# Channel mix's key and value weights split earlier, beside the first cross attention batch, with the receptance product put first

## The reference, cut to what matters

```python
# cross attention (layer 4), each of the 8 batches by itself
q = query @ Wq + bq; k = key @ Wk + bk; v = value @ Wv + bv
attn = softmax((q k^T + q rel_k^T) / sqrt(32))
x = (attn v + attn rel_v) @ Wo + bo
# channel mix (second half of layer 5), H = 4 * 512
xc = _ln(x, ln2_g, ln2_b)
xx2 = _shift(xc)
xk2 = xc * cm_k + xx2 * (1 - cm_k)
xr2 = xc * cm_r + xx2 * (1 - cm_r)
kk = square(relu(xk2 @ ffn_Wk.T))      # (tokens, 2048)
kv = kk @ ffn_Wv.T
x = x + sigmoid(xr2 @ ffn_Wr.T) * kv
```

## Time and profile before

| | us |
|---|---|
| median of 3 runs | 1688.79 (1688.48 to 1689.01) |
| the profiled execution | 1689.68 |
| its span, first to last instruction | 1687.9 |
| cross attention, period 0 (units of the first batch) | 541.9 to 633.7 |
| channel mix, from its first product to its last block | 1523.7 to about 1655 |

### The profile page before, as it was taken

How to read it: one execution, slowest core, us unless ns; L and a number is a source line. 1 busy time by engine, 2 the same in 40 slices (tenths; PEclk the granted TensorE clock), 3 DMA queues, 4 the chain that set the end, 5 groups by cost and what they waited for, 6 DMA issues and landing times. The chain is left out here.

```text
span 1687.9 us, 26535 instructions
## 1 busy us (share of the span) xinstructions
PE 1471.6 (87%) x11120; PEld 1060.0 (63%) x11120; DVE 773.1 (46%) x1333; ACT 466.4 (28%) x772; POOL 557.9 (33%) x315
## 2 busy tenths in 40 slices
PE   8788977477988999999999999999998896936796
PEld 3556755243444778778787787788776673415573
DVE  2455279989435341332322323222232315978913
ACT  0323301031111115243242433324243431303302
POOL 6102057656323032122122122231232324617701
PEclk9779975788998999999999999999999998967997
DMA  5300030010101411111111111111012016003000
GB/s 233 149 1 1 0 137 1 0 69 0 75 0 64 147 51 57 52 34 53 39 42 51 39 48 42 38 52 57 30 42 78 22 57 256 0 0 119 1 0 25
DMA packets 50101, 91.29 MB, mean 54 GB/s; under 512 B 28600, under 2 KB 41664, under 8 KB 46912
## 3 DMA queue, kind: packets, MB, share of 16 engines
q1 hardware_dynamic: 49984, 89.60, 15.1%
HBM read 79.89 MB, written 9.70 MB: 53 GB/s over the span
## 5 line engine op out<-in xcount | busy, mean ns | idle before, releaser
L1074 POOL TENSOR_TENSOR ctx_hi<-ctx_raw,one 128x1536 fp32r<-128x1536 f32 (+1 forms) x36 | 102.9, 2858 | 617.5 <-DMA ctx_raw<-in_ctx 426.0
L1328 DVE TENSOR_TENSOR V<-PS,vbias 128x512 f32<-128x512 f32 (+1 forms) x104 | 71.9, 691 | 338.0 <-PE PS L1114 337.8
L1256 ACT COPY ET<-PS 128x512 f32<-128x512 f32 (+1 forms) x224 | 129.6, 585 | 299.1 <-PE PS L1170 295.4
L1359 DVE TENSOR_SCALAR_CACHE_REDUCE E<-PS 128x384 f32<-128x384 f32 (+1 forms) x256 | 131.8, 571 | 159.6 <-PE PS L1147 159.0
L1170 PE MATMUL PS<-ident,E 128*128 128x128 f32 (+1 forms) x832 | 127.3, 278 | 8.8 <-ACT ET L1256 8.8
L1077 POOL TENSOR_TENSOR ctx_raw_r<-ctx_raw,ctx_hi 128x1536 fp32r<-128x1536 f32 (+1 forms) x36 | 131.2, 3644 | 2.8
L1114 PE MATMUL PS<-ctx_raw_r,wk_hi 128*128 128x384 f32 (+1 forms) x512 | 128.6, 355 | 0.0
L1114 PE MATMUL PS<-wv_lo,ctx_hi 128*128 128x512 f32 (+1 forms) x416 | 125.9, 405 | 0.0
L1114 PE MATMUL PS<-ctx_hi,wk_hi 128*128 128x384 f32 (+1 forms) x512 | 122.9, 361 | 2.5 <-POOL ctx_raw_r L1077 2.5
L1263 ACT ACTIVATE E<-E,peak 128x1601 f32<-128x1601 f32 x64 | 103.5, 1623 | 64.8 <-DVE peak L1364 64.8
L1114 PE MATMUL PS<-wv_hi,ctx_hi 128*128 128x512 f32 (+1 forms) x416 | 120.5, 411 | 0.8 <-issue 0.8
(11 more groups left out here) (283 smaller groups left out, 2383.3 us busy)
## 6 DMA issues: line engine op xcount, KB each, us to landing
ctx_raw<-in_ctx SPq DMA_DIRECT2D x27, 768.0 KB, 4.4
ctx_raw<-in_ctx_first SPq DMA_DIRECT2D x9, 900.0 KB, 4.6
rel_scr<-rel_out SPq DMA_DIRECT2D x8, 640.0 KB, 3.8
fwk<-in_fwk SPq DMA_DIRECT2D x1, 4096.0 KB, 25.4
fwv<-in_fwv SPq DMA_DIRECT2D x1, 4096.0 KB, 12.7
corr<-rel_scr SPq DMA_DIRECT2D x64, 48.0 KB
p_scr<-E SPq DMA_DIRECT2D x16, 192.0 KB, 2.3
near<-p_scr SPq DMA_DIRECT2D x64, 48.0 KB
```

The lines of the kernel that those rows point to most:

```text
L1074: nc.gpsimd.tensor_tensor(ctx_hi[r][:, :, 0:n], ctx_raw[r][:, :, 0:n], one[:].unsqueeze(1).broadcast_to([P, KC, n]), ALU.mult).then_inc(S[ ...
L1256: nc.scalar.copy(ET[0:n, j % ET_RING, :], src[0:n, :]).then_inc(S["et_out"], 1)
L1328: v.tensor_tensor(V[0:rows, at % V_RING, :], bank(4 + NUMBER[unit] % 2)[0:rows, :], vbias[0:rows, :], ALU.add).then_inc(S["v_out"], 1)
L1359: v.tensor_scalar(E[:, p, k0:k0 + n], bank(r)[:, 0:n], 1.0, None, ALU.mult, ALU.max, accum_out=tops[:, p, c:c + 1]).then_inc(S["s_out"], 1)
```

## The change

The key and value weights of channel mix are no longer split there. They are cut into 32 pieces of 128 x 512 (256 KB each; 16 of keys, 16 of values), and each goes through the first batch's period of cross attention: SP loads it into a ring of four buffers (laid over ET, which is unused until period 1), ACT rounds it, DVE takes its rest, and SP stores both parts to a DRAM tensor, `split_scr`. The load of piece i + 4 waits for both stores of piece i. On ACT and DVE a piece stands in the list ahead of the copies of "its" unit; 26 units have one piece; units 9, 19 and 28 have two, unit 28 the pieces 30 and 31 (`PIECES_AFTER`). On SP pieces 0 to 7 are stored one behind each relative store, 8 to 14 behind `load_ctx(2)`, 15 to 21 behind `load_ctx(3)` and ahead of `load_corr(1)`, 22 to 26 behind `load_ctx(4)` and 27 to 31 behind `load_ctx(5)`. The first use of ET and of YT in period 1 waits for all stores.

In channel mix the parts are loaded: the keys' lo part in `cross_output`, the keys' hi part in four DMAs, and both value parts at the start of the block (12 MB there, in place of 4 MB). ACT, DVE and POOL lose their splits, the mix for receptance is made first, and PE makes the receptance product ahead of the 16 groups.

```diff
@@ -901,6 +901,8 @@
 
 
 PERIODS = [(p, p - 1, period(p)) for p in range(B + 1)]
+PIECES, PIECE_RING = 2 * HC, 4
+PIECES_AFTER = [range(i * PIECES // len(UNITS[0]), (i + 1) * PIECES // len(UNITS[0])) for i in range(len(UNITS[0]))]
...
@@ -912,6 +914,7 @@
 
 
 
+    s.split_scr = nc.dram_tensor("split_scr", [2, PIECES, P, D], F32, kind="Internal").ap()
...
+    et_at = m.at
...
+    yt_at = m.at
     s.YT = m.tensor("YT", [P, KC, TOK])
+    over_et, over_yt = Region(nc, et_at), Region(nc, yt_at)
+    piece_raw = over_et.tensor("piece_raw", [P, PIECE_RING, D])
+    piece_lo, piece_hi = over_et.rounded("piece_raw"), over_yt.tensor("piece_hi", [P, PIECE_RING, D], F32R)
...
+
+    def load_piece(sp, i):
+
+        r = i % PIECE_RING
+        if i >= PIECE_RING:
+            sp.wait_ge(piece_stored[r], 32 * (i // PIECE_RING))
+        src = s.dram["fwk"][:, i].rearrange("p c n -> p (c n)") if i < HC else s.dram["fwv"][:, i - HC]
+        sp.dma_start(piece_raw[:, r, :], src).then_inc(piece_loaded[r], 16)
+
+    def store_piece(sp, i):
+
+        r = i % PIECE_RING
+        sp.wait_ge(S["piece_hi"], i + 1)
+        sp.dma_start(s.split_scr[0, i], piece_hi[:, r, :].bitcast(F32)).then_inc(piece_stored[r], 16)
+        sp.wait_ge(S["piece_lo"], i + 1)
+        sp.dma_start(s.split_scr[1, i], piece_lo[:, r, :].bitcast(F32)).then_inc(piece_stored[r], 16)
+        if i + PIECE_RING < PIECES:
+            load_piece(sp, i + PIECE_RING)
...
+            for i in range(PIECE_RING):
+                load_piece(sp, i)
             for b in range(B):
                 sp.wait_ge(S["rel_out_act"], 2 * (b + 1))
                 sp.wait_ge(S["rel_out_dve"], 2 * (b + 1))
                 sp.dma_start(rel_scr[b].rearrange("a p k -> p a k"),
                              rel_out[b % 2][:].rearrange("p o r k -> p (o r) k")).then_inc(rel_stored[b % 2], 16)
+                for i in PIECES_AFTER[b]:
+                    store_piece(sp, i)
             load_corr(sp, 0)
             sp.wait_ge(S["p_zeroed"], 16)
+            stored = PIECES_AFTER[B - 1][-1] + 1
             for p, ba, items in PERIODS:
                 for c in range(NCH):
                     q = p * NCH + c
                     if 2 <= q:
                         load_ctx(sp, q)
+                    if p == 0 and c >= 2:
+                        for i in range(stored, stored + 7):
+                            store_piece(sp, i)
+                        stored += 7
+                    if p == 1 and c < 2:
+                        for i in range(stored, (stored + PIECES) // 2 if c == 0 else PIECES):
+                            store_piece(sp, i)
+                        stored = (stored + PIECES) // 2
                     if ba >= 0 and c == {B - 1: 3, B: 2}.get(p, 1):
                         exchange_near(sp, ba)
                     if c == 3 and p + 1 < B:
@@ -1253,6 +1294,9 @@
                 act.wait_ge(S["t_ps"], T_GROUPS * b + j + 1)
                 if b * P_GROUPS + kt >= 2:
                     act.wait_ge(S["pv_done"], b * P_GROUPS + kt - 1)
+                elif j == 0:
+                    for r in range(PIECE_RING):
+                        act.wait_ge(piece_stored[r], 32 * (PIECES // PIECE_RING))
                 nc.scalar.copy(ET[0:n, j % ET_RING, :], src[0:n, :]).then_inc(S["et_out"], 1)
 
...
+            def piece_round(i):
+                r = i % PIECE_RING
+                act.wait_ge(piece_loaded[r], 16 * (i // PIECE_RING + 1))
+                nc.scalar.copy(piece_hi[:, r, :], piece_raw[:, r, :]).then_inc(S["piece_hi"], 1)
+
             for p, ba, items in PERIODS:
                 for kind, k in items:
+                    if p == 0 and kind == "u" and k % 2:
+                        for i in PIECES_AFTER[k // 2]:
+                            piece_round(i)
...
+                if b == 0:
+                    for r in range(PIECE_RING):
+                        dve.wait_ge(piece_stored[r], 32 * (PIECES // PIECE_RING))
...
+            def piece_rest(i):
+                r = i % PIECE_RING
+                dve.wait_ge(S["piece_hi"], i + 1)
+                v.tensor_tensor(piece_lo[:, r, :], piece_raw[:, r, :], piece_hi[:, r, :].bitcast(F32),
+                                ALU.subtract).then_inc(S["piece_lo"], 1)
+
             for p, ba, items in PERIODS:
                 for kind, k in items:
+                    if p == 0 and kind == "u" and k % 2:
+                        for i in PIECES_AFTER[k // 2]:
+                            piece_rest(i)
                     if kind == "u" and k % 2:
                         unit = UNITS[p][k // 2]
                         if unit[0] == "v":
@@ -1407,6 +1471,7 @@
     s.b8 = Region(nc, nc.sbuf_usable_end // 32 * 32 - 4 * HC * KC * P)
...
 def cross_output(nc, sem, s, nm, nm2):
...
-            sp.dma_start(s.fwk[:], s.dram["fwk"]).then_inc(s.loaded["fwk"], 16)
+            sp.dma_start(s.fwk_lo[:].bitcast(F32).rearrange("p g c n -> p g (c n)"),
+                         s.split_scr[1, 0:HC].rearrange("g p n -> p g n")).then_inc(s.loaded["fwk"], 16)
...
+    fwk_lo, fwk_hi = s.fwk_lo, m.tensor("fwk_hi", [P, HC, KC, P], F32R)
...
-            sp.dma_start(fwv[:], s.dram["fwv"]).then_inc(S["l_v"], 16)
+            for j in range(4):
+                gs = slice(j * GROUP, (j + 1) * GROUP)
+                sp.dma_start(hidden_hi[:, gs].bitcast(F32), s.split_scr[0, gs].rearrange("g p n -> p g n")).then_inc(l_k[j], 16)
+            sp.dma_start(fwv_hi[:].bitcast(F32), s.split_scr[0, HC:PIECES].rearrange("g p n -> p g n")).then_inc(l_v_hi, 16)
+            sp.dma_start(fwv_lo[:].bitcast(F32), s.split_scr[1, HC:PIECES].rearrange("g p n -> p g n")).then_inc(l_v_lo, 16)
...
-            nc.gpsimd.memset(one[:], 1.0).then_inc(S["one"], 1)
             tr.pool(pool, xa, diff)
-            pool.wait_ge(S["one"], 1)
-            pool.wait_ge(S["l_v"], 16)
-            for g in range(HC):
-
-                nc.gpsimd.tensor_tensor(fwv_hi[:, g], fwv[:, g], one[:].broadcast_to([P, D]), ALU.mult).then_inc(S["v_split"], 1)
-                pool.wait_ge(S["v_split"], 2 * g + 1)
-                nc.gpsimd.tensor_tensor(fwv_lo[:, g], fwv[:, g], fwv_hi[:, g].bitcast(F32), ALU.subtract).then_inc(S["v_split"], 1)
...
         @block.tensor
         def _(pe):
             tr.tensor(pe, nm)
+            pe.wait_ge(s.loaded["fwr"], 16)
+            pe.wait_ge(S["mixed_r"], KC)
+            pe.wait_ge(tr.ready, KC)
+            for t in range(NT):
+                linear_to_tokens(nc, bank(t), flat(xr[:]), t, s.fwr, 0, D).then_inc(S["r_ps"], 1)
+            pe.wait_ge(s.loaded["fwk"], 16)
             pe.wait_ge(S["x_lo"], KC)
             for g in range(HC):
-                pe.wait_ge(S["k_lo"], g + 1)
+                pe.wait_ge(l_k[g // GROUP], 16)
...
-            pe.wait_ge(s.loaded["fwr"], 16)
-            pe.wait_ge(S["mixed"], 2 * KC)
-            pe.wait_ge(tr.ready, KC)
-            for t in range(NT):
-                linear_to_tokens(nc, bank(t), flat(xr[:]), t, s.fwr, 0, D).then_inc(S["r_ps"], 1)
-            pe.wait_ge(S["v_split"], 2 * HC)
+            pe.wait_ge(l_v_hi, 16)
+            pe.wait_ge(l_v_lo, 16)
             pe.wait_ge(S["h_lo"], HC)
...
         @block.scalar
         def _(act):
             tr.scalar(act, xa)
-            act.wait_ge(s.loaded["fwk"], 16)
-
-            def key_weights(g):
-                nc.scalar.copy(fwk_hi[:, g], fwk[:, g]).then_inc(S["k_hi"], 1)
...
-            for g in range(AHEAD):
-                key_weights(g)
             for c in range(KC):
                 act.wait_ge(S["mixed"], c + 1)
                 nc.scalar.copy(xk_hi[:, c], xk[:, c]).then_inc(S["x_hi"], 1)
+            for t in range(NT):
+                act.wait_ge(S["r_ps"], t + 1)
+                nc.scalar.activation(gate[:, t, :], bank(t), ACT.Sigmoid).then_inc(S["gate_in"], 1)
...
-                if g + AHEAD < HC:
-                    key_weights(g + AHEAD)
...
                     round_hidden(g - 1)
             round_hidden(HC - 1)
-            for t in range(NT):
-                act.wait_ge(S["r_ps"], t + 1)
-                nc.scalar.activation(gate[:, t, :], bank(t), ACT.Sigmoid).then_inc(S["gate_in"], 1)
...
-            def key_weights(g):
-                dve.wait_ge(S["k_hi"], g + 1)
-                v.tensor_tensor(fwk_lo[:, g], fwk[:, g], fwk_hi[:, g].bitcast(F32), ALU.subtract).then_inc(S["k_lo"], 1)
-
...
+            tr.vector(dve, xa, diff, ((vec("cm_r"), xr),), S["mixed_r"])
             tr.vector(dve, xa, diff, ((vec("cm_k"), xk),), S["mixed"])
-            for g in range(AHEAD):
-                key_weights(g)
             for c in range(KC):
...
-            tr.vector(dve, xa, diff, ((vec("cm_r"), xr),), S["mixed"])
...
-                if g + AHEAD < HC:
-                    key_weights(g + AHEAD)
```

(2 more changed lines are left out.)

10 lines of the change are left out of this document (6 added, 4 removed).

## The result

The changed kernel takes 1772.72 us (median of 4 runs, 1772.19 to 1775.88) against 1688.9 before (4 runs, 1688.48 to 1689.2): ratio 1.05, interval 1.0482 to 1.0519, slower by 84 us. The forecast was 1751, the range 1726 to 1782. The profiled execution took 1775.88, with a span of 1774.1; against the profiled execution of before (span 1687.9) that is 86.2 more, and it is these 86.2 that the traces have to account for.

What follows compares the result with a forecast made beforehand. The prediction took PE to bound period 0, DVE beside POOL channel mix, and SP to become period 0's bound. 1689.68 + 74.0 + 2.7 - 14.5 = 1751.9, given as 1751 for the median; range 1726 to 1782.

Steps and rivals of the forecast that it cites:

- Channel mix: Channel mix without its splits: value product starts at 1596.5, not 1611.00, a gain of 14.5 us, bounds 10 and 16.3.
- the receptance product after an idle PE: Channel mix, PE: 32 products now ahead of the groups take 16.57 us, as time mix's output product did, not 13.89.
- the last hidden parts: Channel mix: the value product must wait for them, uncovered now that the receptance product comes earlier, 3.3 us.
- DVE is left with two of about 0.7 us: Channel mix: DVE drops from three instructions per group to two, 1.4 us per group, so PE's 2.80 us pace counts.
- SP's cycle: Period 0, SP: two store issues, landing wait and load issue take 3.8 us per piece, bounds 3.1 and 4.8; SP becomes the bound.
- steps 3 and 4: Period 0, SP: load_ctx(2) and stores 8 to 14 end at 631.1; load_ctx(3) and stores 15 to 21 at 660.1.
- Steps 6 and 7: End of period 0's batch: 4.6 us from landing to first exponential at 694.5, then unit 30 at 710.2; loss 74 us.
- the trap: End of period 0's batch: pieces 30 and 31 stand behind eight exponentials, 13.1 us, and ahead of unit 28's V copy.
- Step 8: Behind unit 30's wait: PE restarts at half clock after 13 us idle, 2.7 us more; later periods win nothing back.
- (a): Period 0, SP: store landings hide, cycle up to 2.0 us, only step 7's 14 us left; 1688, no change; chance 0.04.
- (b): Period 0, PE: half clock all through, work adds to waits, some 20 us more, 1771; chance 0.12.
- (c): Period 0, SP: a shorter chain, each landing better overlapped than counted; 1729, the lower bound; chance 0.13.

Runs made afterwards that it cites:

- e7: Changed kernel with only the value weights split early, 16 pieces respread over units, loads one piece later, keys split in channel mix as before: 1683.59 us, 0.9961 of the kernel before.
- e6: Changed kernel with the receptance product, its mix and its sigmoid put back behind the 16 groups: 1771.41 us, ratio 1.0483 to the kernel before.
- e3: Changed kernel with both stores of a piece taking rows of x, so no load waits for a store to land: 1717.01 us, ratio 1.017 to the kernel before.
- e5: Changed kernel with the load of piece i + 4 issued behind the stores of piece i + 1 on SP: 1719.94 us, ratio 1.018 to the kernel before.
- e4: Changed kernel without rounding and rest of pieces 30 and 31, their loads and stores kept: 1757.48 us, ratio 1.0417 to the kernel before.
- e10: Kernel before with only the changed channel mix; parts tensor filled with rows of x beside periods 1 to 7, no pieces: 1677.47 us, ratio 0.9933.

## Why the prediction was right, point by point

**Sign and range** held, and the mechanism was the one named: SP's queue, not shares of busy time. The point forecast was 22 us low. In profiled executions the sum of 1751.9 stands against 1775.9, and 21.9 of these 24.0 were there at the first exponential, all by one term.

**Channel mix.** Forecast a gain of 14.5 between bounds of 10 and 16.3; measured 13.9. Its terms: the receptance product after an idle PE 16.57, measured 16.99; groups 2.80 apart, measured 2.80; the last hidden parts 3.3, measured 2.88 idle. "DVE is left with two of about 0.7 us" gave the right number with a reason that was only partly right: e7 keeps the third operation and has the same stage. What slowed DVE was POOL (684 ns per operation without it, 1524 in the median beside it). The prediction named both and did not tell them apart. It also missed that PE is slower behind the last idle time (1.1 us) and that the new order by itself brings nothing (e6). The loads cost nothing, as forecast: 8 MB more, read at up to some 410 GB/s, landed before they were wanted.

**SP's cycle: the term that was too small.** "A cycle is 3.8 us" with a wait of 2.6 behind the issue; plain cycles took 4.3 to 4.4, with 3.1 of wait, and there were longer ones, up to 7.4 behind a context load; 28 waits sum to 102.9 us, 3.7 each. The forecast built the wait from a store that lands alone, 1.9, plus a transfer by rate; the landing with three transfers in flight was 3.3 and 3.6. With the context load's share, the seven stores of steps 3 and 4 took 4.9 us each, where 4.1 was forecast and 5.1 was the upper bound; the 98 us that went with that bound compare with the 95.9 measured. By the steps: 8 turns of 6.5 us (forecast 5.7, bound 6.5) to 599.5 where 592.3 was forecast; `load_corr(0)` cheaper than before, 8.2, so 607.9 for 602.1; stores 8 to 14 to 643.1 for 631.1; stores 15 to 21 to 677.6 for 660.1; `load_corr(1)` 8.3, 686.0 for 670.1; the last load that counts at 709.0 for 687.7. e3 and e5 show that it is the standing still: without it 57 to 59 us of the first exponential's 83 are gone.

The Trainium skill ("DMA: Bandwidth & Descriptors", "Latency and other measured facts") says that a DMA's fixed cost is mostly the answer from the memory it writes to, and that HBM answers in 0.2 us on average but in up to 2 us at high load. The trace agrees in direction: 1.9 us behind the issue for a store by itself, 3.1 here, with the landing growing to 5.5 us in e3 (below). No run here separates the memory's answer from the time behind other transfers.

**Steps 6 and 7, the end of the batch.** Forecast 4.6 us from the landing to the first exponential and 15.7 from there to unit 30; measured 7.4 from the issue of the load (2.2 + 4.6 forecast) and 15.6. e4 gives the trap by itself: 15.2 us in the total.

**Step 8**, half clock behind the idle time: forecast 2.7, measured 2.8. (The two bounds, 1729 and 1778, leave it out.) Not foreseen, since the prediction put period 1 and all behind it at nothing: 2.7 more in the last period, where the clock was granted at 0.89 in 1433 to 1463 and at 1.00 in the same stretch before. It isn't the pieces' doing alone: e10, which has none, shows 0.94 in 1334 to 1364 and is 2.1 us longer there. Its cause stays open; the kernel before has one trace only.

**Rivals.** (a) needed a cycle of at most 2.0 us. With the landing waits taken out e3 reached 2.0 to 2.1, and still lost 29 us to before; the rival would have been wrong even on its own condition, since beside the second trap it counted nothing for the order of SP's list and for the traffic. (b) had the right sight, PE at 0.60 to 0.87 of full clock from 613 to 700, and would have given nearly the measured time, 1771, by 20 us that it didn't work out. But e5 gives the clock back by moving a wait on SP. In the changed kernel itself SP waited 7.1 us for ACT and DVE against 102.9 for landings: the low clock lay inside SP's cycles and set next to nothing; the nearness of its number was chance. (c), the shorter chain, did not happen.

## What to carry to other kernels

A wait for a store's landing, placed between the issues of a queue that others depend on, stops the whole queue every time round (here 3.7 us, 28 times); put the reuse of the buffer one turn later in the list before looking for bandwidth. Before moving work off an engine that is slow beside another, ask which of the two has to go: here taking away one engine's work (POOL's) brought the whole gain, and with that done the other's (DVE's) was carried through DRAM for nothing. Work that is free by shares still needs a place in each in-order list that holds nobody up: not ahead of a context load, not behind eight exponentials and ahead of the copy that PE waits for.

## What the runs showed of the hardware that was not expected

**A landing depends on what is in flight.** The same store of 256 KB to DRAM took 2.2 us from issue to landing by itself (0.3 of issue and 1.9 of wait), 3.3 to 3.6 in the changed kernel at 140 to 230 GB/s, 4.2 to 4.8 in e5, and 5.5 in e3, where slices of 44 us move up to 295 GB/s and the DMA engines are full for some 10 us at a time. The page of e3 (DMA issues, median us to landing):

```profile
split_scr<-X SPq DMA_DIRECT2D x64, 256.0 KB, 5.5
```

The kernel with the slowest landings is also the one with the shortest cycle: only where a wait stands tells what a landing costs.

**DVE beside POOL.** Two-operand fp32 operations of 128 x 512 take 675 to 695 ns in the traces of the changed kernel and of e7, where POOL does not run beside them, and 1524 in the median where it does. The Trainium skill ("SBUF — State Buffer", "SBUF: two separate sides") describes a pair of ports that DVE and POOL share, given to one for a whole instruction while the other stands; the trace agrees in what it shows. In period 0 the pieces' rests take 692 ns in the median and 2924 at most, that one at 697.60, beside a POOL operation of 4.00 us that began at 695.98.

**Reading from DRAM is fast in bulk.** The first 24 us of channel mix move 362 GB/s with the DMA engines at 0.98, and single slices of 2 us show 410 and more (timeline of the DMA engines in 1620 to 1700, GB/s by slice):

```profile
GB/s 0 0 26 314 376 385 391 399 410 410 402 410 410 410 410 410 414 395 409 308 17 0 0 0 0 0 0 0 0 0 8 0 0 0 0 0 0 0 0 0
```

The forecast had 38 us for the 12 MB by the rate of the old value load; the last of them landed 35.3 us after the stage's start (issued at 1629.00, 30.5 to landing).
